# Head operands loaded by row halves, and expert blocks fetched in two parts

## What is computed

```python
xn = _layernorm(x)
s = attention(xn)        # 16 heads of 16, causal, ALiBi bias, softmax
g = _silu(ffn(xn))       # 8 experts, the top 2 of each token, GLU, two matmuls
x = x + s * g
```

## Time and profile before

| | |
|---|---|
| median of 3 runs | 820.03 us (818.52 to 823.14) |
| profiled execution | 815.3 us, of which the span is 813.5 us |
| busy in the span | PE 678.5, DVE 601.9, ACT 475.5, POOL 279.3 us |
| DMA | 85.84 MB, mean 106 GB/s |

### The profile page before, as it was taken

One profiled execution on the slowest core, in us unless ns is written; L12 is line 12 of the kernel. 1 busy time (PEld: TensorE's weight loads), 2 busy tenths in 40 slices (PEclk: granted clock), 3 DMA queues, 4 the chain that ended last, 5 costly groups with the idle time before them and its releaser, 6 DMA issues.

```text
span 813.5 us, 14740 instructions
## 1 busy us (share of the span) xinstructions
PE 678.5 (83%) x5306; PEld 312.0 (38%) x5306; DVE 601.9 (74%) x1222; ACT 475.5 (58%) x990; POOL 279.3 (34%) x458
## 2 busy tenths in 40 slices
PE   3478859769889888989898898889898989898885
PEld 1234545433233433444344444443443443232432
DVE  5999776689777786787678777867886788688342
ACT  2276685860566575666565665666565656666551
POOL 2313442027723323333323433233333234660112
PEclk9889889985899999999999999999999999799998
DMA  9710324634450453244233323522442221350001
GB/s 293 251 65 0 97 73 160 200 130 149 161 145 1 124 152 87 71 124 125 72 86 127 93 74 111 148 83 79 134 127 72 80 90 46 88 185 14 27 32 47
DMA packets 76852, 85.84 MB, mean 106 GB/s; under 512 B 34169, under 2 KB 60284, under 8 KB 76412
## 3 DMA queue, kind: packets, MB, share of 16 engines
q1 hardware_dynamic: 71114, 74.05, 30.0%
q0 software_dynamic: 3280, 8.98, 3.5%
q10 hardware_dynamic: 2386, 1.87, 0.8%
HBM read 39.54 MB, written 27.53 MB: 82 GB/s over the span
## 4 chain that ended last, share of the span: by engine, by line
PE 55%; ACT 18%; DVE 13%; issue 7%; ACTq 3%; DMA 2%; SPq 1%; POOL 1%; POOLq 0%; DVEq 0%
PE bank L1575 16%; ACT PR L830 11%; PE bank L1511 9%; PE bank L1469 8%; DVE PM L1233 5%; PE bank L1534 5%; PE bank L1483 4%; PE bank L1341 3%; ACTq L811 3%; PE bank L1589 2%; PE bank L1384 2%; PE bank L1614 2%; ACT TG L788 1%; ACT U L819 1%; DMA qk_parts<-TG 1%
## 5 line engine op out<-in xcount | busy, mean ns | idle before, releaser
L830 ACT ACTIVATE PR<-bank 128x512 f32<-128x512 f32 (+3 forms) x640 | 317.1, 537 | 226.0 <-PE bank L1534 127.4
L1233 DVE TENSOR_REDUCE PM<-bank 128x1 f32<-128x512 f32 (+3 forms) x640 | 354.3, 604 | 73.6 <-PE bank L1511 46.4
L1534 PE MATMUL bank<-OPS 57*128 57x512 f16 (+3 forms) x640 | 209.6, 363 | 53.4 <-ACT PR L830 48.3
L1511 PE MATMUL bank<-OPS 54*128 54x512 f16 (+3 forms) x640 | 195.8, 372 | 10.5 <-DVE PM L1233 7.0
L1575 PE MATMUL bank<-PR,VS 128*17 128x512 f32 (+3 forms) x1280 | 161.2, 556 | 0.0
L1511 PEld LDWEIGHTS bank<-OPS 54*128 54x128 f16 x640 | 50.2, 95 | 129.6 <-DVE PM L1233 86.9
L1534 PEld LDWEIGHTS bank<-OPS 57*128 57x128 f16 x640 | 54.0, 94 | 117.6 <-ACT PR L830 109.1
L1469 PE MATMUL bank<-WB 128*128 128x256 f16 x552 | 81.2, 277 | 0.0
L600 POOL CAST POSB<-YT 128x256 f16<-128x256 f32 x46 | 18.2, 396 | 173.8 <-DVE YT L1135 173.8
L1469 PEld LDWEIGHTS bank<-WB 128*128 128x128 f16 x552 | 48.2, 98 | 32.5 <-issue 25.9
L1544 PE MATMUL bank<-MASK 64*128 64x64 bf16 x512 | 59.5, 199 | 0.0
(11 more groups left out here) (185 smaller groups left out, 893.2 us busy)
## 6 DMA issues: line engine op xcount, KB each, us to landing
WB<-W SPq DMA_DIRECT2D x23, 512.0 KB, 3.6
OPS<-qk_parts SPq DMA_DIRECT2D x60, 192.0 KB
x_rows<-PR SPq DMA_DIRECT2D x23, 256.0 KB, 3.3
WB<-in_w SPq DMA_DIRECT2D x23, 256.0 KB, 3.5
y_rows<-XT SPq DMA_DIRECT2D x23, 256.0 KB, 3.0
W<-in_w SPq DMA_DIRECT2D x6, 512.0 KB, 5.7
XT<-in_b SPq DMA_DIRECT2D x23, 128.0 KB, 3.9
XO<-in_x SPq DMA_DIRECT2D x4, 512.0 KB, 13.0
```

The source lines that it names most:

```text
L830: act.activation(PR[:, tile % RING, off:CH], PS[2 + tile % 2][:, off:CH], ACT.Exp, scale=1 / SCORE).then_inc(b_exped, 1)
L1233: dve.tensor_reduce(PM[:, c % 2, j, xq, gg:gg + 1], bank[:, 0:width], AX.X, ALU.max).then_inc(a_reduced, 1)
L1511: last = mm(bank[:, 0:width], OPS[ROWS_A, slot, 0, P * (TC * a + xq):P * (TC * a + xq) + P], OPS[ROWS_A, slot, 1, CH * gg:CH * gg + width] ...
L1534: last = mm(bank[:, off:CH], OPS[ROWS_B, slot, 1, P * k:P * k + P], OPS[ROWS_B, slot, 0, CH * b + off:CH * b + CH], start=True, stop=k < T ...
```

## The change

The four DMA groups of a pair (half 0 of its two heads, then half 1 of both) are issued one by one at steps 80p + 4, 24, 48 and 68 of SP's order. Half 0 waits for pass A of the pair that used the slot (`a_scored`), half 1 for pass B (`b_scored`) and is counted on a semaphore of its own, `opb_in`. `fetch_block` loses its two bias DMAs, stands 24 steps ahead of its block and waits for the `up` matmuls of block b - 2 (`up_ps`) and for the split of its second weights (`w2_low`), no longer for its finished output. The biases have a function of their own, 10 steps ahead, which reads the expert's number once more. Three semaphores of the start are folded into others.

```diff
-FETCH_AT = {n - 20: b for n, b in BLOCK_AT.items()}
+FETCH_AT = {n - 24: b for n, b in BLOCK_AT.items()}
+FETCH_BIAS_AT = {n - 10: b for n, b in BLOCK_AT.items()}
+LOAD_AT = {PER_PAIR * p + at: (2 * p + 2 + r, half) for p in range(PAIRS - 1)
+           for half, r, at in ((0, 0, 4), (0, 1, 24), (1, 0, 48), (1, 1, 68)) if p or half}
...
-            def load(h):
-
-                for half in range(2):
-                    load_rows(h, half, opa_in[h // 2 % 2])
-                    load_parts(h, half, slice(0, S), opa_in[h // 2 % 2])
+            def load_half(h, half):
+
+                p = h // 2 - 1
+                if p:
+                    sp.wait_ge((a_scored, b_scored)[half], PER_PAIR * p)
+                if half and h % 2 == 0:
+                    wait(sp, opb_in, 16 * 2 * 3 * p)
+                done = opb_in if half else opa_in[h // 2 % 2]
+                load_rows(h, half, done)
+                load_parts(h, half, slice(0, S), done)
...
-            load(2)
-            load(3)
+            load_half(2, 0)
+            load_half(3, 0)
...
                 if b >= 2:
-                    sp.wait_ge(ye_copied, b - 1)
+                    sp.wait_ge(up_ps, 4 * (b - 1))
+                    sp.wait_ge(w2_low, b - 1)
...
-                sp.dma_start(B2B[:, par, :], b2[ds(e, 1), :].broadcast_to([P, D])).then_inc(block_in[par], 16)
-                sp.dma_start(BB[:, par, :, :].unsqueeze(1), B1S[:, ds(e, 1), :, :]).then_inc(block_in[par], 16)
...
+            def fetch_biases(b):
+
+                par = b % 2
+                if b >= 2:
+                    sp.wait_ge(ye_copied, b - 1)
+                if b == 0:
+                    sp.wait_ge(b1_prep, 3)
+                wait(sp, biases_in, 32 * b)
+                e = sp.value_load(EXPERT[0:1, b:b + 1], min_val=0, max_val=E - 1)
+                sp.dma_start(B2B[:, par, :], b2[ds(e, 1), :].broadcast_to([P, D])).then_inc(biases_in, 16)
+                sp.dma_start(BB[:, par, :, :].unsqueeze(1), B1S[:, ds(e, 1), :, :]).then_inc(biases_in, 16)
...
-                p, rest = divmod(n - LEAD - 1, PER_PAIR)
-                if rest == 0 and 1 <= p < PAIRS - 1:
-                    sp.wait_ge(b_scored, PER_PAIR * p)
-                    load(2 * p + 2)
-                if rest == 8 and 1 <= p < PAIRS - 1:
-                    load(2 * p + 3)
+                if n in LOAD_AT:
+                    load_half(*LOAD_AT[n])
...
+                if tile % PER_PAIR == 0:
+                    wait(pe, opb_in, 16 * 2 * 3 * p)
```

More of the change, by code:

```diff
@@ L316, in build @@
         opa_in = [sem("opa_in0"), sem("opa_in1")]
+        opb_in, biases_in = sem("opb_in"), sem("biases_in")
         parts_out = [sem(f"parts_out{m}") for m in range(4)]
@@ L319, in build @@
         last_in = [sem("last_in0"), sem("last_in1")]
-        ones_in, rows_in, second_in = sem("ones_in"), sem("rows_in"), sem("second_in")
+        second_in = sem("second_in")
         mrow = [sem(f"mrow{s}") for s in range(NC)]
@@ L408, in _ @@
             for h in range(2):
-                load_rows(h, 0, rows_in)
+                load_rows(h, 0, first_in[0])
             for c in range(NC):
@@ L427, in _ @@
                 sp.dma_start(OPS[ROWS_MAX, h, 1, :].rearrange("j (q t) -> j q t", q=NT),
-                             UNITS[:, :].unsqueeze(1).broadcast_to([3, NT, P])).then_inc(ones_in, 16)
+                             UNITS[:, :].unsqueeze(1).broadcast_to([3, NT, P])).then_inc(second_in, 16)
             for h in range(2):
@@ L446, in fetch_block @@
                     sp.wait_ge(w1l_done, E)
-                    sp.wait_ge(b1_prep, 3)
                 e = sp.value_load(EXPERT[0:1, b:b + 1], min_val=0, max_val=E - 1)
@@ L464, in _ @@
                     fetch_block(FETCH_AT[n])
+                if n in FETCH_BIAS_AT:
+                    fetch_biases(FETCH_BIAS_AT[n])
                 if n - 1 in STORE_AT:
                     store_block(STORE_AT[n - 1])
-                p, rest = divmod(n - LEAD - 1, PER_PAIR)
-                if rest == 0 and 1 <= p < PAIRS - 1:
-                    sp.wait_ge(b_scored, PER_PAIR * p)
-                    load(2 * p + 2)
-                if rest == 8 and 1 <= p < PAIRS - 1:
-                    load(2 * p + 3)
+                if n in LOAD_AT:
+                    load_half(*LOAD_AT[n])
             sp.wait_ge(b_scored, TOTAL - PER_PAIR)
@@ L584, in split_weights @@
                 raw = W2B[par]
-                pool.wait_ge(block_in[par], 80 * (b // 2 + 1))
+                pool.wait_ge(block_in[par], 48 * (b // 2 + 1))
                 if b >= 2:
@@ L784, in gate_tanh @@
                 if f == 0:
-                    act.wait_ge(block_in[b % 2], 80 * (b // 2 + 1))
+                    act.wait_ge(biases_in, 32 * (b + 1))
                     if b >= 2:
@@ L1464, in up @@
                     if f == 0:
-                        pe.wait_ge(block_in[b % 2], 80 * (b // 2 + 1))
+                        pe.wait_ge(block_in[b % 2], 48 * (b // 2 + 1))
                     wait(pe, y_ready, 2 * b + f)
@@ L1500, in score_a @@
                 if p == 0 and tile == OFF[c]:
-                    pe.wait_ge(rows_in, 16 * 2)
-                    pe.wait_ge(first_in[c], 16 * 2 * 2)
+                    pe.wait_ge(first_in[c], 16 * 2 * 2 + (16 * 2 if c == 0 else 0))
                 if tile % PER_PAIR == 0:
-                    wait(pe, opa_in[p % 2], 16 * 2 * 2 * 3 * ((p + 1) // 2))
+                    wait(pe, opa_in[p % 2], 16 * 2 * 3 * ((p + 1) // 2))
                 if tile < WIDE:
@@ L1531, in score_b @@
                     if tile == 0:
-                        pe.wait_ge(ones_in, 16 * 4)
-                        pe.wait_ge(second_in, 16 * 2 * 3)
+                        pe.wait_ge(second_in, 16 * 4 + 16 * 2 * 3)
                 last = mm(bank[:, off:CH], OPS[ROWS_B, slot, 1, P * k:P * k + P],
```

## The result

The changed kernel takes 825.35 us (median of 5 runs, 823.3 to 826.36), the kernel before, beside it, 818.52 (5 runs): ratio 1.0073 (1.0041 to 1.0106). The time is inside the range (816.5 to 831).

A forecast was written before the change was run, and what follows sets the result against it. Bound by three engines (PE, ACT, DVE) handing score banks around, not by DMA. All terms 0 except pair 0's 1.1 us stall: 815.3 + 1.1 = 816.4 profiled, 820.0 + 1.1 = 821.1 us median; range 816.5 to 831.

The forecast's parts named there:

- the price of company in pair 0: Pair 0, chunk 3's maxima: other transfers delay their small DMAs by 2.4 us, leaving a 1.1 us stall, once.
- the 1.3 us of room: Chunk 3's maxima, costed in pair 1: they land at 313.8 us, PE needs them at 315.11.
- upper bound of 3.7: Most that neighbouring transfers could delay pair 0's maxima, 3.7 us, from chunk 2 of pair 1; the lower end was 1.2.
- both kinds of neighbour: Pair 0: head operands and a block's fetch both beside the small DMAs, the reason for taking 2.4 us.
- rival A: Pairs 1 to 5: maxima miss a second turn, 1.2 us stall each, perhaps clock falls; 827 to 833 us, chance 0.34.
- The five places: Pairs 1 to 5, chunk 3's maxima beside a fetch: in time with 0.2 us to spare, cost 0.
- the one turn: Pairs 1 to 5: the second small DMA waits once behind the first weights' packets, 1.6 us from the flood's start.
- chunk 0 of pair 2: Earlier trace's model for maxima beside a fetch: second packets 1.6 us after the flood began, 1.2 later than when quiet.
- Split, biases, extra waits: 0: Head loads in halves, biases 18 steps ahead, and added waits on PE, ACT, POOL: each to cost or gain 0.
- Rival B: Faster: head operands had landed late at six pair starts and the split removes that; 815.3 us, chance 0.12.
- the distance: Profiled execution of the kernel before lies 4.7 us below the runs' median; unexplained, carried over to the forecast median.
- Rival C: Early fetches come no earlier, held by `w2_low` or queue order: 820.0 us; no change, with it included, had 0.52.

The follow-up runs named there:

- after_again: The changed kernel run again, unchanged: 826.39 us (8 runs), ratio 1.0079 to the kernel before.
- fetch_held: Changed kernel with block 1's fetch held until pair 0's chunk 3 maxima landed: one run, no ratio given; pair 0's pass B tile 48 is 2.36 us late.
- before_again: The kernel before run again, unchanged: 818.09 us (12 runs), ratio 0.9985; its profiled execution took 814.99 us.
- hold_all: Changed kernel with the next pair's first half load, and the fetch behind it, held until chunk 3's maxima landed, pairs 0 to 5: ratio 0.9985 to the kernel before.
- hold_0: Changed kernel with the first half load and the fetch behind it held until chunk 3's maxima landed, in pair 0 alone: ratio 0.9995 to the kernel before.
- before_third: The kernel before, unchanged, profiled once more: one run, 819.29 us.
- hold_1to5: Changed kernel with the first half load and the fetch behind it held until chunk 3's maxima landed, pairs 1 to 5 only: ratio 1.0061 to the kernel before.
- fetch_only: Changed kernel with early fetch and biases kept, but both halves of a head loaded as in the kernel before: ratio 1.0415 to the kernel before.
- fetch_behind: Early fetch with whole-head loads as in the kernel before, the fetch ahead of the loads moved behind them: ratio 1.0231 to the kernel before.

## Why the prediction was partly right

**Size and class.** Forecast 821.1 and, at 0.52, no change; measured 825.35, slower. By the ratio the change costs 0.73% of about 819, 6.0 us (3.4 to 8.7), where I had 1.1.

**The step that failed: the price of company in pair 0.** "Between ends that far apart I take 2.4 ... leaves a stall of 1.1 us, once." The place, the neighbours and the mechanism were right. The size was not: the stall is 3.0 us, the lag 3.38 and 2.99 in two executions. With the 1.3 us of room the company costs 3.9 to 4.7 us (from the smallest stall, 2.6 in after_again, and the largest lag), above even the upper bound of 3.7. That bound came from chunk 2 of pair 1, and I treated it as an end because pair 0 would have both kinds of neighbour. But chunk 2 had both as well: its small DMAs were issued at 282.16, and the fetch of the earlier trace rows at 282.72, into the head operands. In the kernel before, from 284.3 to 286.2:

```profile
q1 hardware_dynamic: 275, 0.55, 103.9%
q10 hardware_dynamic: 10, 0.00, 0.7%
```

So this row was the like case, to be carried over whole: 3.7 - 1.3 = 2.4 us of stall instead of 1.1. Head operands alone cost as much: 2.36 + 1.3 = 3.7 in fetch_held.

**The term that was missing.** I had the fall of the clock behind a stall in rival A and left it out of the sum. From tile 80 to 160 the changed kernel loses 4.7 us against before_again (5.6 in after_again): 3.4 and 3.0 are the lag, 1.3 and 2.6 the clock behind it. Against the profiled execution of before (72.0 us, with a fall of its own at 248 to 252) it is only 3.5, so a part of this term is chance. All seven profiles with pair 0's stall have a fall behind it. Of the five in which neither pair 0 nor a fetch is late in that stretch (the kernel before three times, hold_all, hold_0), two have one.

**The five places.** "The maxima make it with 0.2 us to spare": they miss by 0.33 to 0.57. The order of issue and the one turn were as forecast; the turn took about 2.1 us from the start of the flood where chunk 0 of pair 2 had 1.6, and the landing 0.6 or more where I had estimated 0.4. So the term 0 of the sum should have been 1.7 us, by the windows of single pairs. It is in keeping with the ratios (1.0061 with these lags cured, 1.0073 and 1.0079 with them), whose intervals are too wide to show it. All three terms give 820.0 + 4.7 + 1.7 = 826.4.

**Split, biases, extra waits: 0.** Right for the change as a whole: with the small DMAs out of the way (hold_all, 0.9985) everything else of it neither costs nor gives anything that shows in its interval (0.9953 to 1.0017). For the parts alone it was wrong: the early fetch without the split costs 4.15%.

**Rival A** had the fault in the wrong place: no second turn in pairs 1 to 5, and no more falls of the clock there than before (the pairs stand at 0.98 or 1.00 in both kernels). Its mechanism, a late landing and the clock behind it, is what happened in pair 0, which I had in the sum already at a quarter of its price. **Rival B** is refuted: before_third is an execution of 819.29 us with pairs no longer than those of 814.99. In this one execution near the median, the distance, "which no view explains", lies in the last stage and is the clock. No head operand was late at a start of pairs 1 to 7. One was in pair 0, whose first 80 tiles took 56.6 us all the same, against 56.5 in before_again.

**Rival C** is refuted by the SP rows of pair 1.

**What stays open.** Of the 10 us between the two profiled spans 3.3 lie ahead of pass A's first tile (177.0 against 180.4 us). Kernels with the same start have 177.1 (hold_0) and 180.2 (hold_1to5), so I count it as chance, without having found its cause. That head operands and small DMAs meet on the same three engines was not seen either, and what the fetch alone would cost in pair 0 no run shows.

## What to carry over

When a transfer is moved, look for the smallest DMA with a deadline near its new place, and price its company by the row of the trace that has the same neighbours, not by a value between two. Then add what the clock takes behind a stall of a few microseconds, here 1.3 to 2.6 us on 3.0 to 3.4. When stretches are compared, take pairs with the same granted clock: that showed 0.3 us a pair where medians showed nothing. And try the parts of such a change alone before they are judged: an early fetch that costs 4% alone cost little once the loads were spread out, and one wait at the right place (hold_0) took most of the loss away, though no version came out faster than the kernel before.

## What was unexpected of the hardware

- A small DMA can be late out of proportion to the load. In fetch_held the second one of pair 0 is issued at 241.2 and its last packets start at about 246.1, 4.9 us later, with SP's queue at 18.1% of the engines' time (241.2 to 246.6). In a quiet stretch it is 1.4 us.
- The issue of a DMA can hold its queue. The transposing DMA took 1.45 us in a quiet queue, 4.94 in the changed kernel's pair 0, 7.42 in fetch_only and 9.37 in fetch_behind, and the issues behind it are late by as much.
- The same ten tiles of the last stage take 12.0, 14.9 or 16.4 us at clocks of 1.00, 0.77 and 0.69 in executions of the same or nearly the same program. In the two executions of the kernel before that stand above, this and the row behind it make more than the whole distance, and a single profile of each side would have charged it to the change.
